# PV and the split of its result one slot later, and a slot's mask ahead of the softmax shift on GpSimd

## The reference

```python
x = x + _layernorm(attn(_layernorm(x)))
x = x + _layernorm(ffn(_layernorm(x)))
# attn: 16 heads of 32, sliding window 256
scores = jnp.einsum('bhnqd,bhnkd->bhnqk', qb, kw) * scale
valid = (t <= s_ + W) & (t >= s_ + 1) & (n * W - W + t >= 0)
scores = jnp.where(valid, scores, NEG)
out = jnp.einsum('bhnqk,bhnkd->bhnqd', jax.nn.softmax(scores, axis=-1), vw)
# ffn: 512 -> 2048 -> 512, ternary weights with row scales, plus a low-rank part of rank 16
h = _bitlinear(x, w_fc) + gate * (x @ v.T @ fast_b.T @ u.T)
r = jnp.maximum(h, 0.0)
out = _bitlinear(r * r, w_proj)
```

## Time and profile before

| | us |
|---|---|
| median of 3 runs (lowest to highest) | 2813.81 (2812.89 to 2814.02) |
| profiled execution, its own time | 2813.22 |
| its span | 2811.5 |
| busy in the span: PE, DVE, ACT, POOL | 2395.4, 1833.2, 1711.9, 1313.0 |

### The profile page before, as it was taken

The page is one execution under the profiler, slowest core; times in us unless marked ns, Lnnn a source line. Parts: engine busy times, 40 slices in busy tenths (PEclk is TensorE's granted clock), DMA queues, the critical chain, the costliest instruction groups (busy, mean ns, idle before and its releaser), DMA issues.

```text
span 2811.5 us, 67929 instructions
## 1 busy us (share of the span) xinstructions
PE 2395.4 (85%) x20892; PEld 1706.4 (61%) x20892; DVE 1833.2 (65%) x4503; ACT 1711.9 (61%) x4357; POOL 1313.0 (47%) x2474
## 2 busy tenths in 40 slices
PE   2468988888988989888988889889888989988987
PEld 2346666666666666666666666666666666666654
DVE  7446666666667666666766666676666666666664
ACT  5256665666656666566656666566665666566661
POOL 1125444455544545454554454455454445445453
PEclk8679999999999999999999999999999999999999
DMA  5011111111111111111111111111111111111100
GB/s 189 24 47 38 35 44 38 36 43 38 46 33 46 37 35 41 42 41 40 40 36 41 42 42 36 43 40 34 44 37 46 35 45 37 35 44 39 37 22 16
DMA packets 151374, 118.66 MB, mean 42 GB/s; under 512 B 31424, under 2 KB 121536, under 8 KB 150480
## 3 DMA queue, kind: packets, MB, share of 16 engines
q1 hardware_dynamic: 150992, 114.05, 14.6%
HBM read 46.83 MB, written 16.78 MB: 23 GB/s over the span
## 4 chain that ended last, share of the span: by engine, by line
PE 45%; issue 19%; DVE 14%; POOL 10%; ACT 7%; DVEq 1%; ACTq 0%; POOLq 0%; SPq 0%; DMA 0%
PE Ab L765 12%; PE F L856 9%; PE F L829 8%; PE Cb L765 4%; DVE Sm L1009 3%; PE Ob L755 3%; PE S L712 3%; PE Tb L738 3%; DVE lnst L1026 2%; POOL sq L1233 2%; POOL PT L1216 2%; ACT Sm L906 2%; POOL x L1228 2%; DVE r L1112 1%; ACT r L964 1%
## 5 line engine op out<-in xcount | busy, mean ns | idle before, releaser
L1009 DVE CUSTOM_DVE_ANT_0 Sm<-S,mask,scales 128x384 f32<-128x384 f32 (+2 forms) x1024 | 574.7, 564 | 574.2 <-PE S L712 561.1
L906 ACT ACTIVATE Sm<-Sm,nmax 128x384 f32<-128x384 f32 (+2 forms) x1024 | 586.7, 573 | 571.0 <-DVE nmax L1009 568.4
L920 ACT ACTIVATE PT<-Tb,one,scales 128x384 f32<-128x384 f32 x896 | 599.2, 669 | 381.7 <-PE Tb L738 377.5
L829 PE MATMUL F<-x2T,t 128*128 128x256 f16 x4096 | 498.2, 276 | 13.4 <-ACT r L964 11.7
L856 PE MATMUL F<-t,r 128*128 128x512 f16 x2048 | 485.2, 380 | 2.4 <-ACT r L964 2.2
L829 PEld LDWEIGHTS F<-x2T,t 128*128 128x128 f16 x4096 | 399.2, 99 | 78.0 <-ACT r L964 27.4
L1233 POOL TENSOR_TENSOR sq<-r 128x512 f32<-128x512 f32 x256 | 289.6, 1131 | 323.6 <-ACT r L964 314.7
L765 PE MATMUL Ab<-xT,w_attn 128*128 128x256 f16 x3072 | 384.6, 276 | 44.4 <-ACT qk L941 42.0
L1185 POOL TENSOR_TENSOR lnrs<-lnve,nhalf 128x1 f32<-128x1 f32 x256 | 153.0, 598 | 472.1 <-DVE lnve L1123 253.8
L765 PEld LDWEIGHTS Ab<-xT,w_attn 128*128 128x128 f16 x3072 | 292.4, 99 | 104.6 <-ACT qk L941 59.1
L738 PE MATMUL Tb<-QK 128*128 128x256 f16 (+1 forms) x1792 | 298.5, 248 | 44.3 <-DVE QK L1018 29.2
(11 more groups left out here) (165 smaller groups left out, 3206.9 us busy)
## 6 DMA issues: line engine op xcount, KB each, us to landing
QK<-qkp SPq DMA_DIRECT2D x1536, 32.0 KB, 1.9
xa<-in_x SPq DMA_DIRECT2D x64, 256.0 KB, 2.7
x<-in_x SPq DMA_DIRECT2D x64, 256.0 KB, 2.8
out<-yc SPq DMA_DIRECT2D x64, 256.0 KB, 2.1
stage<-in_w_fc SPq DMA_DIRECT2D x4, 1024.0 KB, 10.0
stage<-in_w_proj SPq DMA_DIRECT2D x4, 1024.0 KB, 5.8
stage<-in_Wq SPq DMA_DIRECT2D x1, 1024.0 KB, 5.7
stage<-in_Wk SPq DMA_DIRECT2D x1, 1024.0 KB, 8.6
```

The lines of the kernel that those rows point to most:

```text
L829: pe.matmul(Fb[b][:, half * STEP:(half + 1) * STEP], W["t1"][:, k, mc * P:(mc + 1) * P], x2T[:, part, k, :], start=(half == 0 and k == 0 a ...
L906: act.activation(blk, blk, ACT.Exp, bias=nmax[:, hg % 2, j % 8:j % 8 + 1], scale=-1.0, accum_out=sums[:, hg % 2, j % 8:j % 8 + 1]).then_in ...
L920: act.activation(PT[:, n % NPT].rearrange("p b n -> p (b n)"), Tb[:, 0:WIN], ACT.Exp, bias=W["one"][:], scale=W["c"][:, 12:13]).then_inc(M ...
L1009: v.tensor_tensor_reduce(Sm[:, j % NSM, c0:WIN], Sb[j % 2][:, c0:WIN], W["mask"][:, c0:WIN], W["c"][:, 3:4], 3e38, ALU.add, ALU.min, nmax[ ...
```

## The change

The lags of the PV and of the split of its result go up by one each, so that the PVs fall into the slots 1, 5, ... 29 and `out_hi` and `out_lo` into the slots 22, 30, 6 and 14. On POOL the mask of a slot is written ahead of the shift instead of behind it; that matters in the slots 0, 8, 16 and 24, which have both.

```diff
 LAG_LSE, LAG_SHIFT = 1, 3
-LAG_T, LAG_MASK, LAG_PV, LAG_OT = 11, 12, 13, 14
+LAG_T, LAG_MASK, LAG_PV, LAG_OT = 11, 12, 14, 15
...
             def body(it):
                 for s in range(SLOTS):
+                    ok, t, p, i = lagged(it, s, LAG_MASK)
+                    if ok and tile_of(p, i):
+                        mask_tile(t, p, i)
                     ok, t, p, j = lagged(it, s, LAG_LSE)
                     if ok and j % 8 == 7:
                         shift_parts(t, j // 8)
-                    ok, t, p, i = lagged(it, s, LAG_MASK)
-                    if ok and tile_of(p, i):
-                        mask_tile(t, p, i)
```

## The result

| | us |
|---|---|
| before, median of 4 runs (lowest to highest) | 2813.57 (2812.89 to 2814.02) |
| after, median of 4 runs | 2851.72 (2843.19 to 2856.97) |
| ratio, 95% interval | 1.0133 (1.0107 to 1.0158) |
| profiled execution after, its span | 2853.14, 2851.4 |

The change makes the kernel 1.3% slower, 38 us, where I forecast 9 us faster. The time lies above the forecast range, which ended at 2828; the slowest of my cases stood at 2826.

What follows compares the result with a forecast made beforehand. No engine alone was taken as the bound: PE in stretches, a chain across engines in others. 31 steps 0.2 us shorter (6.2) plus 2.9 for the mask order gave 9 us off, 2805 us; range 2788 to 2828.

Steps and rivals of the forecast that it cites:

- the slowest of my cases: Rival: DVE loses the port shared with POOL, +0.5 us a step instead of -0.2, giving 2826 us; chance 0.17.
- slots 21 to 25: QK of slot 24 starts 0.65 us earlier, then the PV in slot 25 costs 0.86: offset +0.2.
- 28 to 30: QK of slot 28 keeps +0.2, the PV in slot 29 adds 0.86, 0.6 is given back: offset +0.5.
- Slots 13 to 19: Output projection in slot 15 waits 0.65 us more for out_lo; given back by slot 19, offset 0.0.
- Slots 21 to 30: QK of slot 24 at -0.65 us, +0.2 behind the PV of slot 25, +0.5 behind slot 30.
- the 0.6: In slot 30 the low-rank product no longer waits for z_last behind out_lo: 0.6 us given back.
- Slots 0 to 9: DVE's chain: masked scores of slot 6 come 1.7 us earlier, out_lo then stands in slot 6; offset at slot 9 -0.2.
- lose the port: Rival in slots 0 to 9: POOL's square starts first and blocks DVE, +0.5 us a step, 2826 us; chance 0.17.
- The mask order: Mask ahead of the shift on POOL saves 0.41 us at each of 7 loop branches, 2.9 us in all.
- The signs named: L755's waits under 10 us, QK's up 40 or more, projection's about 0.6 a step, out_lo's idle over 90, cast 0.42.

Runs made afterwards that it cites:

- e1_fill16: The changed kernel with 16 products of 128x128x256 that nobody reads on PE ahead of QK in slots 24 and 28: 2795.81 us, ratio 0.9948 to the kernel before.
- e12_late_hg012: The kernel before with the split of head groups 0, 1 and 2 one slot later, group 3 left in slot 13: 2720.38 us, ratio 0.9681.
- e9_late_hg2: The kernel before with the split of head group 2 alone one slot later, slot 6 in place of 5: 2774.38 us, ratio 0.9873.
- e4_split_only: The kernel before with the split of OT alone one slot later, PVs and mask order as they were: 2745.66 us, ratio 0.9774.
- e2_lags_only: The kernel before with both lags raised, mask behind the shift as before: 2842.77 us, ratio 1.0119.

## Why the prediction was wrong

- **The step that failed** is in slots 21 to 25, and again in 28 to 30: "taking the PV away frees nothing here; PE idles from 1554.3 on". The second half was true, and I put the cost of that idle time at zero. It is not free when it comes in one piece: 1.02 us of wait, 0.86 of PV and 0.47 of wait held the clock, and 2.16 us of wait let it fall, for 3.41 us, which costs about 1.6. The changed kernel has 29 such stretches more than before, some 46 us, in a time that is 38 us longer. e1_fill16 shows it: with the hole filled and all else left, 56 us come back.
- No case of mine had the clock in it. I had read that it was at nine tenths or more and took it for a constant. The mean of 0.973 in the line of the core is not 1, and the steps with p = 0, which already lack the PV of slot 24, had the undivided wait, the fall behind it and 80.4 us instead of 78.7. I had noted that a PV is absent there, and did not look at these steps.
- **Slots 13 to 19**: right where p is not 0. The wait came at 0.58 against 0.65, and was given back at slot 19 but for 0.16. Where p is 0 it is not given back (0.72); I had counted all steps alike.
- **Slots 21 to 30**: the path was right. QK of slot 24 came at -0.61 against -0.65, the PVs in slots 25 and 29 cost 1.82 against 1.72, and the 0.6 came back in slot 30 (e12_late_hg012).
- **Slots 0 to 9**: right in the changed kernel. I had the masked scores of slot 6 at 1.7 us earlier and those of slot 7 at -0.2; in e1_fill16 they are at -1.71 and -0.24. The cast did come out at 0.42, so DVE did not lose the port:

```profile
1617.10 0.42 DVE L1112 CAST r<-sq 128x512 f16<-128x512 f32 x1
...
1617.94 1.20 POOL L1233 TENSOR_TENSOR sq<-r 128x512 f32<-128x512 f32 x1 [0.97 <-ACT r L964]
```

  From slot 5 to slot 13 that is a gain of 0.84, where my offsets have 0.7. With the PVs left in their slots (e9_late_hg2, e4_split_only) the late split of group 2 gives 1.3: 0.6 up to slot 7 (0.8 here), and 0.7 more at slots 8 and 9 (0.1 here), which I had not followed.
- **The mask order**: wrong, nothing in two comparisons. The 0.41 us on POOL is real and the 0.97 of wait on the first transpose was too, but the gain does not reach the end.
- **The signs named** came true: the waits of L755 gone, those of QK up by 99 us, the projection's wait of 0.6 us a step (19.5 in all), out_lo's idle time over 90 (131.6), the cast at 0.42, the scores' wait for the shift's copy down from 29.2 to 17.5 us. They tell that the order of events was understood. None of them could have told of the clock, because each was a wait, and what the clock takes shows in busy time.

So the path was worked out rightly and the time was not: of the 9 us forecast 6.2 were the lags', 0.2 a step, and e1_fill16 has 0.19; the 2.9 of the mask order were not there; and the clock, which stood in no term, took more than all of it. The sum of the lags also held two large parts that I never set apart. The late split of OT is a gain of 64 us by itself, and the PVs of slots 24 and 28 out of their wait are a loss of 98, of which 59.5 are the clock's.

## What to carry to other kernels

Work that lies in a long wait of PE is not only free, it may be what keeps the clock: before moving it away, ask how long PE then stands idle in one piece and what it must do right after, and compare the durations of one form before and after. If two parts of a change move together only because they are numbered together, work each out alone; here one half was worth 64 us and the other half took more than that. If a piece of work cannot be had to put there, useless products in the wait may pay: here they gave back 56 us, and where the wait was already parted they gave nothing. And where some steps of the kernel before already lack the piece of work, as those with p = 0 did here, they show what its absence does: look at them first.

## What the runs showed of the hardware

- The granted clock fell to 0.50 for 3.41 us behind undivided idle times of PE of 2.16 and 2.29 us, in a kernel whose PE is busy for 86% of its span. Of the idle times over 1.9 us 41 of 68 were followed by such a fall; in the kernel before four falls stood behind 1.69 us.
- Such a stretch made a step 1.4 to 1.7 us longer (81.61, 83.05 and 84.62 us with none, one and two in e2_lags_only; 78.7 and 80.4 before), or cost nothing (81.61 and 81.61 before, with none and one).
- At half of the clock the twelve products of QK took 2.70 and 2.47 us instead of 1.48, and the PVs that began as the stretch was ending 0.94 and 1.17 instead of 0.86.
- 16 products of 128x128x256 in the hole, 1.91 us in all, kept it at 1.00, as did one PV of 0.86 us, with idle times of 1.02 and 0.47 on either side.
